# Two graph layers on one core: VectorE reads the base nodes into registers just ahead of the additions that use them

## What is computed

```python
def layer0(x, edge_index, W, b):          # a graph convolution
    row, col = edge_index
    deg = segment_sum(ones, col) + 1.0
    dis = rsqrt(deg)
    h = x @ W
    agg = segment_sum(h[row] * (dis[row] * dis[col])[:, None], col)
    agg = agg + h * (dis * dis)[:, None]
    return x + gelu(agg + b)

def layer1(node_x, edge_x, sources, targets, ...):
    m = concat(node_x[sources], node_x[targets], edge_x)
    message = relu(m @ msg_W1 + msg_b1) @ msg_W2 + msg_b2
    agg = segment_sum(message, targets)
    return relu(concat(agg, node_x) @ upd_W1 + upd_b1) @ upd_W2 + upd_b2

x = x + layer0(relu(layernorm(x)), (src, dst), ...)
x = x + layer1(relu(layernorm(x)), edge_attr_64, src, dst, ...)
```

## Time and profile before

| | us |
|---|---|
| median of 3 runs | 2400.13 |
| lowest and highest run | 2398.8, 2419.97 |
| the profiled execution, its own time | 2400.34 |
| its span, from the first to the last instruction | 2398.6 |
| busy in the span: TensorE | 2151.4 |
| VectorE | 1698.6 |
| GpSimd | 1631.1 |
| ScalarE | 1129.7 |

### The profile page before, as it was taken

One profiled execution on the slowest core, in us unless ns is written; L12 is line 12 of the kernel. 1 busy time (PEld: TensorE's weight loads), 2 busy tenths in 40 slices (PEclk: granted clock), 3 DMA queues, 4 the chain that ended last, 5 costly groups with the idle time before them and its releaser, 6 DMA issues.

```text
span 2398.6 us, 73497 instructions
## 1 busy us (share of the span) xinstructions
PE 2151.4 (90%) x23620; PEld 1934.3 (81%) x23620; DVE 1698.6 (71%) x4585; ACT 1129.7 (47%) x2379; POOL 1631.1 (68%) x1606
## 2 busy tenths in 40 slices
PE   2256899999999838999999999999999999999998
PEld 1144687787787638999999999999999999999995
DVE  8866787787787695666666666666666666666662
ACT  0004787888888643444334444444444334444442
POOL 5375777777777315777777777777777777777771
PEclk6556999999999968999999999999999999999999
DMA  2002111111111122333333333333333333333332
GB/s 73 1 1 44 27 27 29 27 27 27 27 27 28 13 61 58 74 77 74 74 74 73 76 75 74 73 73 73 74 77 74 73 75 73 75 75 73 73 74 35
DMA packets 347320, 134.23 MB, mean 56 GB/s; under 512 B 305390, under 2 KB 322644, under 8 KB 347188
## 3 DMA queue, kind: packets, MB, share of 16 engines
q1 hardware_dynamic: 298356, 82.41, 15.3%
q0 software_dynamic: 48832, 50.10, 12.1%
HBM read 124.84 MB, written 7.52 MB: 55 GB/s over the span
## 4 chain that ended last, share of the span: by engine, by line
PE 79%; DVE 8%; POOL 6%; issue 5%; DMA 1%; DVEq 0%; ACT 0%; SPq 0%; POOLq 0%; PEld 0%; PEldq 0%; ACTq 0%
PE psum L1711 17%; PE psum L1653 14%; PE psum L1725 12%; PE psum L1523 8%; PE psum L1644 8%; PE psum L1554 6%; POOL rows L646 6%; PE psum L1663 5%; PE psum L1689 2%; PE psum L1544 2%; PE psum L1678 1%; PE psum L1490 1%; PE psum L1534 1%; DVE work L792 1%; PE psum L1782 1%
## 5 line engine op out<-in xcount | busy, mean ns | idle before, releaser
L646 POOL DMA_INDIRECT rows<-a_rows,idx x1078 | 1049.5, 974 | 433.7 <-issue 300.1
L646 POOL DMA_INDIRECT rows<-g_rows,idx x448 | 463.3, 1034 | 153.5 <-issue 135.6
L1294 ACT ACTIVATE hT<-psum 128x392 bf16<-128x392 f32 x1120 | 497.1, 502 | 134.0 <-PE psum L1554 125.9
L1523 PE MATMUL psum<-work,hT 128*128 128x192 bf16 x3430 | 445.3, 248 | 0.3 <-ACT hT L1294 0.3
L1711 PE MATMUL psum<-edge_index,H 128*128 128x192 bf16 x4802 | 429.2, 246 | 2.5 <-DVE H L1067 2.4
L1347 ACT ACTIVATE eoT<-psum 128x512 f32<-128x512 f32 x392 | 213.9, 603 | 407.9 <-PE psum L1644 407.9
L1711 PEld LDWEIGHTS psum<-edge_index,H 128*128 128x128 bf16 x4802 | 398.2, 99 | 3.7 <-DVE H L1067 2.5
L1554 PE MATMUL psum<-Z,one_lo 128*128 128x392 f16 x1120 | 358.2, 341 | 26.9 <-DVE Z L908 26.8
L1653 PE MATMUL psum<-wb,eoT 128*128 128x64 f32 x3136 | 376.0, 273 | 0.0
L1523 PEld LDWEIGHTS psum<-work,hT 128*128 128x128 bf16 x3430 | 316.8, 99 | 69.9 <-issue 2.8
L1653 PEld LDWEIGHTS psum<-wb,eoT 128*128 128x128 f32 x3136 | 367.3, 193 | 0.1
(11 more groups left out here) (272 smaller groups left out, 2043.1 us busy)
## 6 DMA issues: line engine op xcount, KB each, us to landing
work<-in_edge_attr_dram SPq DMA_DIRECT2D x390, 128.0 KB
rows<-a_rows,idx POOLq DMA_INDIRECT x1078
Z<-slot_code SPq DMA_DIRECT2D x98, 160.0 KB
rows<-g_rows,idx POOLq DMA_INDIRECT x448
idx<-src_by_tile SPq DMA_DIRECT2D x203, 4.0 KB
wb<-b_rows SPq DMA_DIRECT2D x196, 16.0 KB, 2.1
g_rows<-Y SPq DMA_DIRECT2D x1, 1600.0 KB, 8.9
a_rows<-Y SPq DMA_DIRECT2D x6, 256.0 KB, 2.7
```

Of the source, the lines that this page charges most:

```text
L646: pool.indirect_dma_start(out=rows[:, k, t, :], out_offset=None, in_=table, in_offset=bass.IndirectOffsetOnAxis(ap=idx[:, k, t:t + 1], axis=0)
L1294: nc.scalar.activation(counts[:, j % 2, :, t * SLOTS:(t + 1) * SLOTS], psum[:, t % 4, 0:KEYS].rearrange("p (h m) -> p h m", m=SLOTS), ACT.Copy
L1523: ins = TT.matmul(psum[:, 4 + (j + 1) % 2, 0:NPART * D], counts[:, (j + 1) % 2, h, :], gtab[:, h, :, :].rearrange("p k d -> p (k d)"), sta ...
```

## The change

The reads of the bases move from the start of a step to the place just ahead of the addition that uses them. In layer 1 `g0` is read ahead of the waits of the gathered addition and `b0` ahead of `add_counted`. In layer 2 `b0` is read ahead of `add_sums`. All other instructions stay in their order, and so do the other engines' programs.

```diff
@@ mixed_step (layer 1)
-                if started:
-                    b0 = dve.value_load(base_i[0:1, bass.ds((i * MB + j - 2) * 2, 1)], min_val=0, max_val=NP - BW)
-                if 1 <= j <= MS:
-                    g0 = dve.value_load(base_i[0:1, bass.ds(i * MS + j - 1 + S0, 1)], min_val=0, max_val=NP - W)
                 if j < MS:
                     dve.wait_ge(summed[0], i * MS + j + 1)
                     window_onehots(i * MS + j + S0, onehot0[:, j % U]).then_inc(onehot[0], 1)
...
                 count_onehots(i, j, 1)
                 if 1 <= j <= MS:
+                    g0 = dve.value_load(base_i[0:1, bass.ds(i * MS + j - 1 + S0, 1)], min_val=0, max_val=NP - W)
                     dve.wait_ge(summed[0], i * MS + j - 1 + U + 1)
                     dve.wait_ge(acc_add[0], i * ADDS + place_gathered(j - 1) + 1)
                     V.tensor_tensor(acc[0:D, bass.ds(g0, W)], acc[0:D, bass.ds(g0, W)], psum[0:D, 7, 0:W],
                                     ALU.add).then_inc(acc_add[0], 1)
                 if started:
+                    b0 = dve.value_load(base_i[0:1, bass.ds((i * MB + j - 2) * 2, 1)], min_val=0, max_val=NP - BW)
                     add_counted(i, j, b0, place_counted(j))
@@ message_passes, step (layer 2)
                     def step(i, k, last, before_last=False):
-                        b0 = dve.value_load(base_i[0:1, bass.ds(i * U + k, 1)], min_val=0, max_val=NP - W)
                         if not last or k + 3 < U:
                             onehots_of(*ahead(i, k, 3))
                         add_rows(i, k)
...
+                        b0 = dve.value_load(base_i[0:1, bass.ds(i * U + k, 1)], min_val=0, max_val=NP - W)
                         add_sums(i, k, b0)
```

## The result

The changed kernel took 2431.15 us (median of four runs, 2431.01 to 2432.86); the kernel before, run beside it, 2399.47 us (four runs, 2398.2 to 2419.97). The ratio is 1.011, 95% interval 1.0078 to 1.0142: slower by about 1%. The prediction was 2400.0 us with a range to 2409. Further runs on two other chips gave 1.0085 (1.0051 to 1.0119) and 1.0101 (1.0064 to 1.0137).

A forecast was written before the change was run, and what follows sets the result against it. TensorE was taken to bound both layers' loops, except a gather-bound stretch and the loop's turns in layer 1. From 2400.34 us, 0 each for layer 2, the end and layer 1 gave 2400.3, written as 2400.0; range 2394 to 2409.

The forecast's parts named there:

- the last one on layer 1: Layer 1's gathers: the shift of VectorE's gaps was taken to change their time by 0 us.
- the slow rival: Layer 1: closer comparisons meet more gathers, 1.5 us in the gather-bound stretch plus 13.3 later, 2415 us in all; chance 0.11.
- Layer 2, 0 us: Layer 2's loop: VectorE saves 69 us, which becomes longer waiting for TensorE at the additions; 0 us on the path.
- the 0.3 us of new idle: Layer 2, additions that no wait stops: the moved read delays each by some 0.3 us, covered by 5.6 us.
- The end, 0 us: End of layer 2: the last step's read moves behind the message addition, beside other work; 0 us both ways.
- Layer 1's comparisons, 0 us: Layer 1: comparisons come up to 1.4 us sooner, but the saved time becomes a wait for TensorE's buffer; 0 us.
- What sets layer 1's pace: Layer 1's loop: TensorE sets the pace, except gathers from 236 to 300 us and stands at the loop's turns.
- the bound stretch: Layer 1 from 236 to 300 us, where the chain lies on GpSimd's gathers; slower gathers cost at once, 1.5 us.
- The spare time of 2.1 us: Layer 1's later bodies: gathers could run 2.1 us longer over a body's eight gathered steps before they decide.
- The fast rival: Turns of layer 1's loop: a 0.7 us read goes at six turns, 4.2 us, plus 2.4 from gathers, 2393 us; chance 0.07.
- the cases of 0.82, 0.07 and 0.11: Whole kernel: unchanged pace, 2398 to 2402 us (0.82); faster, 2393 to 2397 (0.07); slower by gathers, mostly 2403 to 2415 (0.11).

The follow-up runs named there:

- e1: Kernel before with only layer 1's two reads moved; 2423.25 us, ratio 1.0084 to the kernel before.
- e3: Changed kernel with layer 1's two reads also kept at the step's start, into unused registers; 2402.63 us, ratio 1.0017 to the kernel before.
- e2: Kernel before with only layer 2's read moved; 2399.51 us, ratio 1.0019 to the kernel before.
- e15: Changed kernel run again unaltered, on another chip; 2445.38 us, ratio 1.0101 to the kernel before.
- e4: Changed kernel run again unaltered, on another chip; 2434.38 us, ratio 1.0085 to the kernel before.
- e13: Kernel before with layer 1's two reads one place later, between the targets' one-hots and the first half of the comparisons; 2406.49 us, ratio 0.9948.
- e6: Kernel before, with VectorE waiting for its own fourth comparison ahead of the fifth in each half; 2405.70 us, ratio 0.9942.
- e5: Changed kernel, with VectorE waiting for its own fourth comparison ahead of the fifth in each half of layer 1's comparisons; 2425.74 us, ratio 1.0026 to the kernel before.
- e7: Kernel before with only layer 1's b0 read moved, g0 staying at the step's start; 2403.13 us, ratio 0.9949.

## Why the prediction was wrong

The step that failed is the last one on layer 1: "I take 0, since VectorE's gaps are moved, not closed." It was the ground on which the slow rival was given 0.11. What the runs showed in its place: the pause ahead of the one-hots was closed, the gathers' busy time grew by 17.3 us, and the loop with it by 18.8 (e1 alone has it, e3 takes 14.6 of it back).

- **Layer 2, 0 us: right.** The additions' stand and the 0.3 us of new idle are there, and the loop is the same within 0.2 us (e2: 1.0019). Only the place was wrong: about 59 us more of waiting stand at line 1083, none at the additions. A comparison that follows the addition sooner does not make that addition wait longer; it makes VectorE early for the next thing that it takes from TensorE.
- **The end, 0 us: right.** The rest of the time after the last sums is 1.0 us shorter.
- **Layer 1's comparisons, 0 us: wrong.** I had read the wait of the earlier trace rows (1.37 us at line 905 for TensorE) as the place to which the pause would go. That row is from the stretch at TensorE's pace. In the stretch at the gathers' pace TensorE's buffers are free early, so VectorE has nothing to wait for between line 921 and the end of the eight comparisons, and the pause was closed. At the step of 228 us the kernel before has 0.57 us of issue idle and no other pause in it. Where the waits do return, they stand behind the comparisons (37.1 us at line 915), too late for the gather that started ahead of them.
- **What sets layer 1's pace: half right.** "So both loops run at TensorE's pace, with two exceptions" holds for the later bodies of before, by some 2 to 4 us only. That GpSimd is filled for 399.6 of 400 us stood in the earlier trace rows, and was not taken as a second pace.
- **The slow rival: right direction, mis-sized in its parts.** I had priced it as half as many collisions again at the sizes seen: 1.5 us in the bound stretch, 13.3 in later bodies. Instead a few gathers were held for most of a chain, which the trace of before could not show: 3.7 us extra for the one at 228.72, where the largest extra in before was 1.8. The first two bodies lost 18.7 us. The later bodies, which I had thought the costly part, lost 0.1 over all. The spare time of 2.1 us that I had worked out is seen once: body 3 took two held gathers (4.00 and 3.88 us), its gathers 3.8 us more in all, and the sums' distance from the gathers fell from 3.7 to 1.7 us, with no loss in the body. In bodies 4 to 6 nothing had to fit, as the gathers took 3.3 us less in all in spite of one held in each. With the spare time used up the loss comes at once: body 7's 4.9 us, and in e15 bodies 4 and 5, with two each, took 89.5 and 91.3 us. That the sum of the later bodies came out even in the changed kernel's execution was luck; in e15 they lost 18.5 us. The rival's total, 1.5 + 13.3 = 14.8 us, is near the 18.8 by luck too, as both of its parts are wrong. The price that I had put on the bound stretch, each gather's extra time at once, was the right rule with too small a gather.
- **The fast rival: not shown.** Bodies 4 to 6 begin with a step of 8.58 us where there were 9.7 to 10.1. But in e4, the same kernel, bodies 4 to 6 begin with 8.58, 8.62 and 10.08 us and in e15 with 10.13, 10.08 and 10.12, and in the kernel before body 7 begins with 8.61. In e13, with a pause, bodies 3 to 7 all begin with 8.58. Something else than the reads decides there; it was not tried.
- **The range.** The stretch between the layers was in no term. It can move an execution by 14 us; the highest run of before, 2419.97, was in front of me, and I had not asked what it was. The chances do not add up either: the cases of 0.82, 0.07 and 0.11 make 1.00, and 0.01 for what I did not see and 0.02 for a gain of over 1% came on top.

The Trainium skill's rule (page "SBUF — State Buffer", section "Who interferes with whom") that a two-port VectorE instruction and a GpSimd one exclude each other for their whole length spoke for the slow rival, and the runs agree in direction. It did not say what decided the size here: a chain of VectorE's instructions without a pause keeps GpSimd out for more than one of them, 3.7 us extra at 228.72. Nor do the rows show an exclusion of every pair: the gather at 452.69 of the changed kernel takes 0.94 us while the second half's comparisons run from 451.49 to 453.72. Which of VectorE's instructions here are two-port ones no row says.

## What to carry to other kernels

An idle gap on an engine that is not the bound may be what lets another engine work. Before closing one, look in the stretch where that other engine sets the pace, list the operations on both sides of the gap, and ask what will stand between them then; a wait from another stretch does not count. And a wait on an engine's own work, put in to open a gap, costs the sequencer its lead: one in a half cost next to nothing here (e6: the loop 618.6 us against 619.3), three made VectorE the bound. Where two engines' paces lie within a few us of each other, add up the busy time and the gaps of both over the whole stretch; the chain that ended last names only the one that was ahead at the end.

## What was not expected of the hardware

- A gather of 0.94 us took up to 4.75 us in the changed kernel. Of the 13 held ones eight end 0.12 us after VectorE has fallen idle, two 0.70 and 0.82 us after it and two 0.02 us ahead of it; the longest, from 201.13 us, ends inside a chain of 11.1 us, as one of 2.75 us does in the kernel before at nearly the same place. A pause of 35 ns was enough to let a gather in (e5). Which gathers of a chain are caught, and how some get in without a pause, is open.
- TensorE's clock after the lull between the layers stayed at 0.50 for 44.4 to 47.8 us in seven profiled executions and for 105.8 us in five, at the same place and with the same work ahead. What picks one is open.
- The same program was granted 0.93 to 0.95 of TensorE's clock on average on the chips of e1 to e7 and e13 to e15 and 0.77 to 0.78 on two others, where it took 3858 to 3933 us in place of 2400 to 2423; the layer 1 differences studied here cannot be seen there.
